# Graph attention on one core: three sums per PSUM bank and four batches in flight, and the softmax head's transposes moved from TensorE to VectorE

## What is computed

```
def _gat_layer(x, src, dst, W_i, a_src_i, a_dst_i, b_i):
    h = (x @ W_i).reshape(n, H, C)
    es = jnp.einsum('nhc,hc->nh', h, a_src_i)
    ed = jnp.einsum('nhc,hc->nh', h, a_dst_i)
    e = es[src] + ed[dst]
    e = jnp.where(e > 0, e, NEG_SLOPE * e)
    m = jax.ops.segment_max(e, dst, num_segments=n)
    p = jnp.exp(e - m[dst])
    denom = jax.ops.segment_sum(p, dst, num_segments=n)
    alpha = p / denom[dst]
    msg = alpha[:, :, None] * h[src]
    out = jax.ops.segment_sum(msg, dst, num_segments=n)
    return out.reshape(n, H * C) + b_i
```

## Time and profile before

| | us |
|---|---|
| median of 3 runs | 10107.16 |
| lowest, highest | 10101.89, 10107.39 |
| the profiled execution | 10027.24 |
| its span, first to last instruction | 10025.4 |
| first attention layer, first to last group | 2110.9 to 4566.1 |
| second | 4759.3 to 7215.3 |
| third | 7429.6 to 9842.5 |

### The profile page before, as it was taken

The page is one execution under the profiler, slowest core; times in us unless marked ns, Lnnn a source line. Parts: engine busy times, 40 slices in busy tenths (PEclk is TensorE's granted clock), DMA queues, the critical chain, the costliest instruction groups (busy, mean ns, idle before and its releaser), DMA issues.

```text
span 10025.4 us, 128907 instructions
## 1 busy us (share of the span) xinstructions
PE 5468.7 (55%) x33764; PEld 4402.8 (44%) x33764; DVE 5313.1 (53%) x12476; ACT 4632.0 (46%) x8410; POOL 4936.8 (49%) x5153
## 2 busy tenths in 40 slices
PE   3999799635444444553544445444534444444446
PEld 2777566524444444442444444444423333333334
DVE  5888711335555555554555555555634444444445
ACT  2555300245555555553555555555434444444444
POOL 2000300156666666662666666666466666666660
PEclk9999899855555555555555555555555555555558
DMA  2333355134333333442333333433322222222221
GB/s 83 141 135 141 122 187 191 61 99 108 102 103 101 103 103 103 107 105 66 102 103 102 102 102 104 108 102 103 80 74 76 71 71 71 76 71 71 71 76 32
DMA packets 600500, 985.16 MB, mean 98 GB/s; under 512 B 330886, under 2 KB 454492, under 8 KB 560780
## 3 DMA queue, kind: packets, MB, share of 16 engines
q1 hardware_dynamic: 216924, 540.94, 16.0%
q0 software_dynamic: 163376, 356.21, 15.2%
q10 hardware_dynamic: 219648, 81.82, 3.1%
HBM read 755.78 MB, written 222.74 MB: 98 GB/s over the span
## 4 chain that ended last, share of the span: by engine, by line
PE 30%; DVE 22%; another core or an unknown queue 19%; DVEq 14%; issue 10%; ACT 3%; DMA 1%; ACTq 1%; POOL 0%; POOLq 0%; SPq 0%
PE bank L1040 12%; DVEq L1363 11%; DVE acc L1993 10%; PE bank L1275 8%; DVE arena L1980 3%; PE bank L1064 2%; PE bank L1215 2%; PE bank L1203 2%; DVE bank L1949 2%; DVEq L1993 2%; DVE arena L1951 1%; ACT pick_dist L863 1%; DVEq L1985 1%; PE bank L1346 1%
## 5 line engine op out<-in xcount | busy, mean ns | idle before, releaser
L706 POOL DMA_INDIRECT arena<-row_table,staged_idx x4980 | 4700.9, 944 | 3010.1 <-issue 1749.0
L1275 PE MATMUL bank<-arena 128*128 128x136 f32 x9984 | 2452.2, 424 | 1521.3 <-issue 729.0
L1275 PEld LDWEIGHTS bank<-arena 128*128 128x128 f32 x9984 | 2171.8, 312 | 1688.3 <-issue 1688.2
L1993 DVE TENSOR_TENSOR acc<-acc,bank 128x136 f32 x4992 | 1476.5, 296 | 2096.8 <-issue 822.5
L863 ACT ACTIVATE pick_dist<-col,dst_local 128x128 bf16<-128x128 f32 x4992 | 1521.8, 388 | 551.1 <-remote 419.6
L1040 PE MATMUL bank<-arena 128*128 128x385 bf16 (+1 forms) x7448 | 1325.5, 327 | 36.5 <-DVE arena L1733 20.0
L815 ACT COPY x_mem<-bank 128x384 f32<-128x384 f32 x416 | 198.9, 478 | 1619.1 <-remote 1001.5
L1040 PEld LDWEIGHTS bank<-arena 128*128 128x128 bf16 x7448 | 702.2, 98 | 458.1 <-issue 22.1
L1980 DVE TENSOR_TENSOR arena<-arena,bank 128x528 f32<-128x528 f32 x1248 | 831.9, 687 | 0.7
L648 POOL TENSOR_TENSOR arena<-acc,node_stat 128x896 f32 x14 | 23.9, 1708 | 1612.6 <-POOLq L660 987.5
L1215 PE MATMUL bank<-ident,x_mem 96*128 96x96 f32 x1664 | 365.7, 375 | 738.7 <-DVE x_mem L1641 494.0
(11 more groups left out here) (371 smaller groups left out, 5343.6 us busy)
## 6 DMA issues: line engine op xcount, KB each, us to landing
arena<-dst_rows SPq DMA_DIRECT2D x156, 1024.0 KB
cell_rows<-arena SPq DMA_DIRECT2D x75, 1568.0 KB, 5.1
arena<-cell_rows SPq DMA_DIRECT2D x75, 1568.0 KB, 6.5
edge_stats<-x_mem ACTq DMA_DIRECT2D x416, 192.0 KB
arena<-row_table,staged_idx POOLq DMA_INDIRECT x4980
x_mem<-in_edge_attr SPq DMA_DIRECT2D x208, 192.0 KB
x_mem<-segment_flags SPq DMA_DIRECT2D x416, 96.0 KB
arena<-change_rows SPq DMA_DIRECT2D x312, 64.0 KB
```

The lines of the kernel that those rows point to most:

```text
L706: pool.indirect_dma_start(gathered[:, at, :], None, table, bass.IndirectOffsetOnAxis(staged_idx[:, at:at + 1], 0)).then_inc(att_gathered[n ...
L1275: mm = pe.matmul(region(k)[:, 0:ROW], pick[:, k, :], gathered[:, b * GROUP + k, :], start=True, stop=True)
L1993: done = dve.tensor_tensor(row, row, region(m * BATCH + k), ALU.add)
```

## The change

Three things are changed together.

- A batch is three slots, the last of a group two: 11 batches a group in place of 8. A bank holds the three results of one batch (3 x 136 = 408 of 512 floats), and a batch takes the next of the four banks in turn. So four batches, 12 slots, can be in flight: TensorE begins a batch when the fourth before it has been added. VectorE weighs four batches ahead.
- The head's four transposes on TensorE are gone, with the semaphores `score_rows`, `firsts`, `ends`, `crossed`, `cross_rows`, `maxima` and `max_back`. VectorE turns blocks of 32x32 itself: four instructions for the scores, two for the ends, one for the crossings, four for the maxima. The copy of the crossings out of PSUM (L1943) is gone.
- The head's pieces and the scans of edge attributes stand after other batches, since there are more and smaller ones. TensorE waits for `scored` before it overwrites the destinations' scores.

```diff
-BATCH = 4
+BATCH = 3
+HELD = 4
...
-        def region(k):
-            return bank[:, 4 + k % (2 * BATCH) // 2, k % 2 * ROW:(k % 2 + 1) * ROW]
+        def region(G, m, k):
+            at = k - m * BATCH
+            return bank[:, 4 + (G * NBATCH + m) % HELD, at * ROW:(at + 1) * ROW]
...
-                    pe.wait_ge(att.added, G * STEPS + m + FREE + (1 if m >= 2 else 0))
-                    for k in range(m * BATCH, (m + 1) * BATCH):
-                        mm = pe.matmul(region(k)[:, 0:ROW], pick[:, k, :], gathered[:, b * GROUP + k, :],
+                    taken_group, taken_batch = divmod(G * NBATCH + m - HELD, NBATCH)
+                    if taken_group >= 0:
+                        pe.wait_ge(att.added, taken_group * STEPS + taken_batch + 2)
+                    for k in slots:
+                        mm = pe.matmul(region(G, m, k), pick[:, k, :], gathered[:, b * GROUP + k, :],
...
-                        if head and m == 2 + late:
-                            turn_scores(G + 1)
-                        if head and m == 3 + late:
-                            turn_ends(G + 1)
-                        if head and m == 4 + late:
-                            turn_crossings(G + 1)
-                        if head and m == min(5 + late, NBATCH - 1):
-                            turn_maxima(G + 1)
...
+                def turn_scores():
+                    then()
+                    for q in range(P // GROUP):
+                        dve.transpose(score_rows_h[:, :, q * GROUP:(q + 1) * GROUP],
+                                      score[q * GROUP:(q + 1) * GROUP, :, :])
+                    then()
...
+                    dve.transpose(row_ends[:, 0:GROUP],
+                                  seg_f_h.rearrange("s h e -> s e h")[:, ::-1, :][:, 0:GROUP // HEADS, :])
+                    dve.transpose(row_ends[:, GROUP:2 * GROUP],
+                                  seg_m_h.rearrange("s h e -> s e h")[:, 0:GROUP // HEADS, :])
...
+                    dve.transpose(cross_rows, cross[:, :, :].rearrange("p m s -> p (m s)"))
...
+                def turn_maxima():
+                    then()
+                    for q in range(P // GROUP):
+                        dve.transpose(back[q * GROUP:(q + 1) * GROUP, :, :],
+                                      seg_m_h[:, :, q * GROUP:(q + 1) * GROUP])
+                    then()
...
-                    weigh(G, b, 0)
-                    weigh(G, b, 1)
+                    for m in range(HELD):
+                        weigh(G, b, m)
                     late = 0 if ahead else 3
                     for m in range(NBATCH):
-                        if m + 2 < NBATCH:
-                            weigh(G, b, m + 2)
+                        if m + HELD < NBATCH:
+                            weigh(G, b, m + HELD)
                         add_batch(G, slot, m)
                         if head and m == 0 + late:
                             score_edges(G + 1, 1 - b, use)
-                        if head and m == 1 + late:
-                            first_scans(G + 1, 1 - b, use)
                         if head and m == 2 + late:
-                            carries(G + 1, 1 - b)
+                            turn_scores()
+                            first_scans(1 - b, use)
                         if head and m == 3 + late:
-                            last_scans(G + 1, 1 - b)
-                        if head and m == min(5 + late, NBATCH - 1):
-                            shift_scores(G + 1, 1 - b, slot + GROUP)
+                            carries(1 - b)
+                        if head and m == 4 + late:
+                            last_scans(1 - b)
+                        if head and m == 7 + late:
+                            turn_maxima()
+                            shift_scores(1 - b, slot + GROUP)
```

More of the change, by code:

```diff
@@ L236, in build_graph_network @@
         seg_m = over(2560, GROUP, 512)
+        score_rows = bank[0:GROUP, 3, :]
         raw, score = (over(3584 + n * P, P, HEADS, GROUP) for n in range(2))
+        back = bank[:, 3, 0:P].rearrange("p (h s) -> p h s", h=HEADS)
+        row_ends = over(3840, GROUP, 2 * GROUP)
+        cross_rows = over(3840 + 2 * GROUP, GROUP, 2 * GROUP)
         prob = bank[:, 1, 0:HEADS * GROUP].rearrange("p (h s) -> p h s", h=HEADS)
@@ L391, in build_graph_network @@
         att = sems("att", "staged picked rows_loaded turned dst_scored summed added flags0 flags1 "
-                          "scored score_rows firsts ends crossed cross_rows maxima max_back shifted prob "
+                          "scored shifted prob "
                           "log_scale scale_rows scale weighted used")
@@ L1219, in _ @@
                 if n == 0:
-                    pe.sem_inc(att.added, FREE_REGIONS)
                     pe.sem_inc(st.turned, 2 * FREE)
@@ L1263, in score_some @@
                 def score_some(first, last, slot, turned):
+                    if first == 0:
+                        pe.wait_ge(att.scored, turned // 2)
                     for j in range(first, last):
@@ L1890, in _ @@
             edp = bank[:, 2, 0:GROUP * PARTS * HEADS].rearrange("p (s m h) -> p h s m", m=PARTS, h=HEADS)
-            back = bank[:, 3, BACK_AT:BACK_AT + P].rearrange("p (h s) -> p h s", h=HEADS)
-            grp = bank[0:GROUP, 3, :]
+            score_rows_h, seg_f_h, seg_m_h = (v.rearrange("s (h e) -> s h e", h=HEADS) for v in (score_rows, seg_f, seg_m))
             for n in range(LAYERS):
@@ L1950, in last_scans @@
                     then()
-                    dve.tensor_tensor_scan(seg_m[:, ::-1], end_flag[:, b, ::-1], grp[:, ::-1], FAR,
-                                           ALU.add, ALU.max).then_inc(att.maxima, 1)
-                def shift_scores(head, b, slot):
-                    dve.wait_ge(att.max_back, head + 1)
+                    dve.tensor_tensor_scan(seg_m[:, ::-1], end_flag[:, b, ::-1], score_rows[:, ::-1], FAR,
+                                           ALU.add, ALU.max)
+                def turn_maxima():
+                    then()
+                    for q in range(P // GROUP):
+                        dve.transpose(back[q * GROUP:(q + 1) * GROUP, :, :],
+                                      seg_m_h[:, :, q * GROUP:(q + 1) * GROUP])
+                    then()
@@ L1956, in shift_scores @@
+                def shift_scores(b, slot):
                     dve.tensor_tensor(score[:, :, :], score[:, :, :], back, ALU.subtract
@@ L1958, in shift_scores @@
                     dve.tensor_tensor(log_scale[:, :], cross_rows[0:1, 0:HEADS],
-                                      bank[0:1, 3, BACK_AT:BACK_AT + P:GROUP], ALU.subtract
+                                      back[0:1, :, 0], ALU.subtract
                                       ).then_inc(att.log_scale, 1)
@@ L1989, in add_batch @@
                     dve.sem_inc(dve_tick, 1)
-                    for k in range(BATCH):
-                        row = acc[:, bass.ds(at[k], ROW)]
+                    for k in slots:
+                        row = acc[:, bass.ds(at[k - m * BATCH], ROW)]
                         then()
-                        done = dve.tensor_tensor(row, row, region(m * BATCH + k), ALU.add)
+                        done = dve.tensor_tensor(row, row, region(G, m, k), ALU.add)
                     done.then_inc(att.added, 1)
```

121 lines of the change are left out of this document (45 added, 76 removed).

## The result

The changed kernel took 10304.69 us (median of 4 runs, 10282.3 to 10325.0) beside 10105.1 for the kernel before: ratio 1.0197, interval 1.0176 to 1.0219. The forecast was 10000, faster; the change costs 200 us. The profiled execution has a span of 10280.5 us against 10025.4.

What follows compares the result with a forecast made beforehand. GpSimd's gathers bound the kernel: a floor of 39.8 us a group plus pauses waiting for sums. Terms 0 - 104 - 2 = -106 us take 10027.24 to 9921; plus 79.9 gives 10000, range 9760 to 10340 (forecast's own 9870 to 10090).

Steps and rivals of the forecast that it cites:

- The floor and the price of a pause: GpSimd: a group takes 39.8 us of gathers plus pauses, each 2.2 us after 8 gathers, 3.1 or 3.4 after 16.
- a sign against itself: Profile after: pauses gone without a change in credits would make the reading of held reports, and the whole sum, wrong.
- the reading: TensorE's reports made some 4 to 7 us into a gather run are seen only 1.7 to 3.1 us after it ends.
- VectorE's sum: VectorE's occupied time a group, 34.5 us plus turns and batches, comes to 38.3, still under GpSimd's floor of 39.8.
- The 0.7: VectorE, us a group for more batches: three more weighings at 0.4 in all, with three more address-list reads 0.7.
- The transposes: Turns on VectorE: eight large at 0.28 us plus smaller ones, 2.7 us a group, 3.1 with gaps less the copy.
- rival B: VectorE becomes the bound: transposes at 0.90 us each, +2.3 us a group, +235 us, 10340; chance 0.10.
- Credits: Slots in flight, 12 for 8: 0 us for the first two layers, -104 in the third.
- The gain of the third layer: Third layer's group falls to 45.3 us, between two pauses (46.6) and one (43.4): -2.0 x 52 = -104 us.
- C: Rival: a fourth pause a group, as a burst brings 9 or 6 slots, +180 to +230 us, about 10310; chance 0.18.

Runs made afterwards that it cites:

- aligned_read: The changed kernel, with VectorE reading addresses in eight lists of four a group from multiples of four: 10083.39 us, ratio 1.0021 to the kernel before, held.
- aligned_early: The changed kernel with eight address lists from multiples of four and the next group weighed before the last two adds: 10034.62 us, 0.9974 of the kernel before, held.
- fixed_adds: The changed kernel with VectorE's adds at addresses written in the code, not read, so sums go wrong: 8655.95 us, ratio 1.0000 to the kernel before, prompt.
- The early weighing: The changed kernel, with VectorE weighing the next group's batches before the group's last two adds: alone 8848.77 us, ratio 1.0220 to the kernel before, prompt.

## Why the prediction was wrong

**The floor and the price of a pause.** Right as an account of the time: gathers of 1.25 us and pauses, in every held trace. A burst after a run of 18 comes 3.3 to 3.5 us after it, after 9 2.1, after 5 1.2, on the line of 1.7 after 8 and 2.9 after 16. But the prediction named a sign against itself, pauses that go without a change in the number of credits, and that is what a prompt occasion shows: the kernel before takes 8660 us there, which leaves no room for them (no trace of it was taken there, but that of batches alone has none). So the reading holds for held occasions alone, and says nothing of what makes them.

**The step that failed** is VectorE's sum, "34.5 + 3.1 + 0.7 = 38.3 us, still under 39.8". The 0.7 had three more reads of addresses for some 0.3 us together. I did not look up the read, which stood in VectorE's queue in the trace of before at 0.343 us, since its row carries no busy time; and I took for granted that three addresses cost no more than four. They cost 0.745, and the reads together 5.2 us a group more of VectorE's queue in place of 0.3. By that the sum is 38.3 - 0.3 + 5.2 = 43.2 us, over 39.8. Not all of it is uncovered, as an address is read while the engine still computes: with batches alone and prompt reports the idle time "issue" of the adds is 364.7 us with lists of three and 268.9 with aligned ones, 1.9 us a group. Where reports are held, VectorE so comes late to the end of a group, into the stretch in which each of its small instructions takes 0.7 us.

**The transposes** were priced nearly right. They took 0.315 and 0.322 us for the large ones, 0.219, 0.177 and 0.222 for the small: 8 x 0.319 + 0.62 = 3.2 us against 2.7. The form was taken right, and rival B's price of 0.90 was far off. The Trainium skill's 0.31 for a bf16 block of 128x128 ("VectorE: DVE Perf Modes", "The three transpose paths") was nearer than my 0.28; the trace agrees with it by its number, though for 128 elements of f32 in 32 partitions. What I missed is how little room was left: on a prompt occasion the turns alone cost 130 us.

**Credits.** The count of pauses went as forecast or better: counting those over 1 us, in the first layer 3.4 a group before and 3.1 after, in the third 2.6 and 2.1. The account of the credits had no case for a burst that brings no sum. With twelve slots in flight TensorE finishes its group early, and the next credit then hangs on VectorE: last adds, rescaling, weighing. I priced a pause by the length of its run alone, at most 3.6 us; those after 14 gathers in the third layer have a median of 6.7 (held report 2.8 us after the run, first sum 5.9 us).

**The gain of the third layer** was put too high as well, and would not have come with quick reads either: aligned_read is 0.2% slower than the kernel before, aligned_early 0.3% faster, against a forecast of 1%. Fewer pauses come after longer runs, and each is dearer for it. By the earlier trace rows a pause costs 2.2 us after 8 gathers and 3.4 after 16, 0.15 for each gather more, so that one pause after 32 would cost 5.8, an estimate; I had 3.6. In aligned_early the third layer has runs of 24 and 8 with median pauses of 5.2 and 2.7, and 47.1 us a group. The forecast's 45.3, midway to one pause, was out of reach; of its own range only the end with two pauses, 46.6, was near.

**The rivals.** C gave 10310, and the time was 10305, but its mechanism, a fourth pause, is not what happened: there are fewer pauses and longer ones. B had the right engine and the wrong operation; it was not the transposes. That two parts which each cost nothing could cost 2% together stood nowhere. The sum did set both against one slack, but with the reads at 0.3 us in it both fitted in.

**What stays open.** Why an occasion is held. What makes the change's variants 2 to 3% slower on prompt occasions: reads and register instructions were only left out together there. Whether VectorE's crawl (2.4 to 2.6 us from one add to the next late in a run) costs much by itself: fixed_adds, which would tell, met a prompt occasion, and with aligned reads the crawl is still there (637 instructions of about 0.7 us in the third layer) while the loss is gone. The early weighing was timed with held reports only on top of the aligned reads, where it gave a further 0.5%. A longer gap between gathers was never tried in the form that was meant.

## What to carry to other kernels

When a change makes more and smaller batches, price what a batch costs the engine's queue (address reads, register instructions), not only its arithmetic, and read it from the queue's own rows. In this kernel lists of addresses were read quickest four at a time from multiples of four. When pauses get dearer with the length of the run before them, fewer of them are worth less than their number says. When two parts of a change are each hidden by the slack of one engine, add them up against that slack once; and where engine A restarts on what B and C have ready at one moment, ask what is ready then, not only how many may be in flight.

## What the runs showed of the hardware

- A read of one address into VectorE's registers took 0.31 us, two 0.525, three 0.745, four from a multiple of four 0.343, four from another place 0.965.
- On some occasions, and not by the chip, TensorE's reports made late in GpSimd's run of indirect DMAs are seen only after the run has ended, 1.2 us after it (run of 5), 1.7 (8), 2.9 to 3.1 (16), 3.3 to 3.5 (18), 4.4 (24). Late in such a run VectorE's register instructions take 0.7 us in place of 0.046, and its drains and semaphore waits 0.7 too; on other occasions neither is seen. The kernel before takes some 10070 us on the ones and 8660 on the others.
- A memset of 128x1 and a drain on GpSimd behind each indirect DMA cost 2.2 us: (19617 - 8663) / 4980.
